# Adaptive layer-norm FFN, 1 core: condition slice 0 asked for in halves on two DMA queues, transposes and x tiles between the weight pieces

## The reference

```python
masked_w = weight * mask[None, :, :]                  # weight 8 x 512 x 512
w_bot = jnp.einsum('bg,got->bot', y, masked_w)        # y = cond_8, 2 x 8
h = jnp.einsum('bnt,bot->bno', x, w_bot) + bias
# _weight_quant: scale = 1/mean|w|, round(w*scale) clipped to -1..1, divided by scale
# _act_quant: scale = 127/max|row|, round(x*scale), divided by scale
gate = jax.nn.silu(_bitlinear(h, w_gate))             # 512 -> 2048
up = _bitlinear(h, w_up)                              # 512 -> 2048
return x + _bitlinear(gate * up, w_down)              # 2048 -> 512
```

## Time and profile before

| | |
|---|---|
| median of 3 runs | 454.75 us (453.04 to 455.91) |
| profiled execution, its own time | 453.42 us |
| its span | 451.6 us |
| PE busy | 434.9 us (96%) |
| DVE busy | 366.4 us (81%) |
| ACT busy | 327.1 us (72%) |
| POOL busy | 154.4 us (34%) |
| granted PE clock | full in every slice |

### The profile page before, as it was taken

The page is one execution under the profiler, slowest core; times in us unless marked ns, Lnnn a source line. Parts: engine busy times, 40 slices in busy tenths (PEclk is TensorE's granted clock), DMA queues, the critical chain, the costliest instruction groups (busy, mean ns, idle before and its releaser), DMA issues.

```text
span 451.6 us, 7215 instructions
## 1 busy us (share of the span) xinstructions
PE 434.9 (96%) x2186; PEld 232.7 (52%) x2186; DVE 366.4 (81%) x625; ACT 327.1 (72%) x448; POOL 154.4 (34%) x160
## 2 busy tenths in 40 slices
PE   4899998999999999999999999999999999999995
PEld 0234443444444455555655555655556565555654
DVE  0316579898956798799998999999999989999991
ACT  1216847785356776888888888888888888888861
POOL 0000170606099554232424324233341434414122
PEclk9999999999999999999999999999999999999999
DMA  7999997995420434352634526345353553535455
GB/s 281 402 401 415 412 252 160 339 279 121 102 48 10 78 77 109 103 116 77 159 69 134 119 75 150 67 133 118 91 134 75 141 107 103 116 93 142 86 148 139
DMA packets 104458, 69.78 MB, mean 155 GB/s; under 512 B 87281, under 2 KB 87537, under 8 KB 102897
## 3 DMA queue, kind: packets, MB, share of 16 engines
q1 hardware_dynamic: 103856, 67.39, 54.3%
q10 hardware_dynamic: 576, 2.10, 1.3%
HBM read 40.11 MB, written 8.39 MB: 107 GB/s over the span
## 4 chain that ended last, share of the span: by engine, by line
PE 44%; DMA 23%; DVE 12%; issue 11%; ACT 8%; SPq 1%; DVEq 0%; ACTq 0%
PE ps L888 12%; DMA wc<-wc 12%; PE ps L843 10%; PE ps L951 8%; PE ps L923 7%; DMA wc<-w_gate 4%; PE ps L881 4%; ACT wc L473 4%; DVE wc L733 3%; DVE wc L699 3%; DMA qT<-q_sb 3%; DMA wc<-wcond 2%; DMA wc<-w_down 2%; DVE p_part L751 2%; PE ps L856 1%
## 5 line engine op out<-in xcount | busy, mean ns | idle before, releaser
L888 PE MATMUL ps<-tern_up,qT 128*128 128x512 f16 x512 | 131.2, 379 | 0.6 <-DVE wc L733 0.6
L843 PE MATMUL ps<-w_bot,xT_sb 128*128 128x512 f32 x256 | 113.2, 595 | 2.3 <-DVE w_bot L636 1.6
L843 PEld LDWEIGHTS ps<-w_bot,xT_sb 128*128 128x128 f32 x256 | 48.0, 190 | 61.2 <-issue 57.5
L751 DVE TENSOR_REDUCE p_part<-wc 128x1 f32<-128x1536 f32 x64 | 77.9, 1218 | 1.7
L888 PEld LDWEIGHTS ps<-tern_up,qT 128*128 (+1 forms) x512 | 50.0, 98 | 55.3 <-DVE wc L733 1.3
L733 DVE TENSOR_TENSOR wc<-ps,xT_sb 128x512 f32<-128x512 f32 x104 | 71.3, 685 | 7.5 <-issue 3.6
L473 ACT ACTIVATE wc<-wc 128x1024 f16<-128x1024 f32 x64 | 67.0, 1051 | 4.6 <-DVE wc L796 2.8
L463 ACT ACTIVATE wc<-wc,p_scale 128x2048 f32<-128x2048 f32 x31 | 62.1, 2002 | 4.5 <-DVE p_scale L789 4.5
L951 PE MATMUL ps<-wc 128*128 128x256 f16 x480 | 62.2, 273 | 0.2 <-DVE wc L699 0.2
L699 DVE TENSOR_TENSOR wc<-wc 128x1024 f16<-128x1024 f16 x60 | 56.7, 945 | 3.8 <-DMA wc<-wc 2.7
L458 ACT ACTIVATE xT_sb<-ps,gate_unit 128x512 f32<-128x512 f32 x78 | 49.2, 684 | 11.7 <-PE ps L923 11.2
(11 more groups left out here) (93 smaller groups left out, 544.1 us busy)
## 6 DMA issues: line engine op xcount, KB each, us to landing
xT_sb<-xT SPq DMA_DIRECT2D x32, 256.0 KB, 7.5
x_res<-x SPq DMA_DIRECT2D x30, 256.0 KB, 2.9
out<-result SPq DMA_DIRECT2D x30, 256.0 KB, 2.4
wc<-wcond SPq DMA_DIRECT2D x12, 512.0 KB, 13.6
wc<-w_gate SPq DMA_DIRECT2D x4, 1024.0 KB, 17.7
wc<-w_up SPq DMA_DIRECT2D x4, 1024.0 KB, 13.4
wc<-w_down SPq DMA_DIRECT2D x4, 1024.0 KB, 7.3
wc<-wcond ACTq DMA_DIRECT2D x4, 512.0 KB, 7.7
```

The lines of the kernel that those rows point to most:

```text
L751: nc.vector.tensor_reduce(p_part[:, par, i:i + 1], prod[:, par, 512 * lo:512 * hi], AX.X, ALU.max, apply_absolute_value=True).then_inc(par ...
L843: ins = nc.tensor.matmul(ps[:, t % COND_BANKS], xT_sb[:, t % XSLOTS, k], w_bot[:, t // HALF, k], start=(k == 0), stop=(k == KH - 1))
L888: ins = nc.tensor.matmul(ps[:, UP + i % 2], tile_of(s, k), tern_up[:, i, k], start=(k == 0), stop=(k == KH - 1))
```

## The change

1. ACT asks for pieces 0 and 1 of condition slice 0 alone, and SP for pieces 2 and 3, behind `y_col` and in front of the first mask and the x tiles 0 to 2.
2. SP asks for the x tiles 8 to 10 between w_gate's pieces 1 and 2 (before: behind piece 3). Each of these loads waits for a tile of PE, and gate 2 and 3 are behind them.
3. SP asks for the transposes of tiles 0 to 3 between the pieces of w_up, and for the masks and x tiles 12 to 14 there too (before: masks and x tile 11 between up 1 and 2, all transposes behind up 3). AHEAD is 11 for 12.
4. ACT sums gate 0 and 1, then rounds tile 0, sums gate 2, rounds tile 1, sums gate 3, and rounds tile 2 (before: all four sums first).
5. `abs_total(0)` goes from ahead of tile 8 to ahead of tile 9, and its bank from 2 to 3.

```diff
-AHEAD = 12
+AHEAD = 11
-SUM_TILE = (8, 14, 21)
-SUM_BANK = (10 % 8, 16 % 8, 23 % 8)
+SUM_TILE = (9, 14, 21)
+SUM_BANK = (11 % 8, 16 % 8, 23 % 8)
...
             sp.dma_start(y_sb[:, :], y_col).then_inc(s_small, 16)
+            for i in range(2, 4):
+                sp.dma_start(wc[:, 0, 2 * i:2 * i + 2], wcond[0, :, 2 * i:2 * i + 2]).then_inc(s_wc[0][i], 16)
             load_wc(0)
...
-            for a in range(PIECES):
-                if a % 2 == 0:
-                    sp.wait_ge(mix_psum, 2 * (a // 2 + 1))
-                load_raw(0, w_gate, a)
-            for a in range(PIECES):
-                if a % 2 == 0:
-                    sp.wait_ge(mix_psum, 2 * (a // 2 + 3))
-                if a == 0:
-                    for t in range(XSLOTS, XSLOTS + 3):
-                        load_xT(t)
-                if a == 2:
-                    for k in range(KH):
-                        load_mask(1, k)
-                    for t in range(XSLOTS + 3, AHEAD):
-                        load_xT(t)
-                load_raw(1, w_up, a)
-            for t in range(LATE):
+            sp.wait_ge(mix_psum, 4)
+            load_raw(0, w_gate, 0)
+            load_raw(0, w_gate, 1)
+            for t in range(XSLOTS, XSLOTS + 3):
+                load_xT(t)
+            load_raw(0, w_gate, 2)
+            load_raw(0, w_gate, 3)
+            load_xT(XSLOTS + 3)
+            sp.wait_ge(mix_psum, 2 * KH)
+            load_raw(1, w_up, 0)
+            transpose_q(0)
+            load_raw(1, w_up, 1)
+            transpose_q(1)
+            for k in range(KH):
+                load_mask(1, k)
+            load_xT(XSLOTS + 4)
+            transpose_q(2)
+            load_raw(1, w_up, 2)
+            load_xT(XSLOTS + 5)
+            transpose_q(3)
+            load_raw(1, w_up, 3)
+            load_xT(XSLOTS + 6)
+            for t in range(QSLOTS, LATE):
...
-            for i in range(4):
+            for i in range(2):
                 nc.scalar.dma_start(wc[:, 0, 2 * i:2 * i + 2], wcond[0, :, 2 * i:2 * i + 2]).then_inc(s_wc[0][i], 16)
...
-            for a in range(PIECES):
-                abs_sum_piece(0, a)
-            abs_after = {3: (1, 0), 4: (1, 1), 5: (1, 2), 6: (1, 3), 12: (2, 0), 13: (2, 1), 14: (2, 2), 15: (2, 3)}
+            abs_sum_piece(0, 0)
+            abs_sum_piece(0, 1)
+            abs_after = {0: (0, 2), 1: (0, 3), 3: (1, 0), 4: (1, 1), 5: (1, 2), 6: (1, 3), 12: (2, 0), 13: (2, 1), 14: (2, 2), 15: (2, 3)}
```

## The result

| | before | changed |
|---|---|---|
| median of 12 runs | 453.40 us (452.71 to 455.91) | 455.74 us (453.43 to 457.59) |
| profiled execution, its own time | 453.42 us | 454.06 us |
| its span | 451.6 us | 452.3 us |

The ratio of the times is 1.0046, with a 95% interval of 1.0032 to 1.0060: the changed kernel is slower by 0.46%, about 2.1 us (the medians lie 2.3 us apart). I had forecast a gain of 0.9 us. The profiled execution lies near the lower end of its kernel's runs and shows 0.7 us of it; the other part is looked for in the experiments.

A forecast was written before the change was run, and what follows sets the result against it. DMA was taken as full from 6 to 56 us, PE as leading from 128 us. Front 0, tile 16 -0.55 and `abs_total(2)` -0.33 make -0.9 us: 453.9 us from a 454.75 median, range 451.4 to 457.4.

The forecast's parts named there:

- gate 2 is then issued at 40.8, before gate 1 lands, so the queue need not run empty: DMA queue between w_gate's pieces 1 and 2: no gap; if it ran empty, up to half a microsecond later.
- rival C: Gate pieces: gate 2 lands 1 to 2 us later than 45.6, tile 16 +0.45 to +1.45, 454.9 to 455.9 us; chance 0.12.
- The bytes ahead of gate 2: Three x tiles, 0.79 MB, ahead of gate 2 take 1.9 to 2.0 us, so it lands at 45.6 for 43.6.
- POOL's start: POOL's scaling of w_gate starts 0.55 to 0.6 us earlier, at 54.7 us.
- tile 16: PE's tile 16, which waits for DVE's mean of w_up, starts at 79.24 us for 79.79, -0.55 us.
- The 0.33 us at `abs_total(2)`: PE no longer waits at its last abs_total, near 97 us: -0.33 us.
- the longer stand at this place: PE, ready earlier, stands 1.5 us for the mean of w_up ahead of tile 16 instead of 0.64.
- The front: Condition slices and mixing: PE's head start from slice 0 is spent in waits for slices 1 and 2; gain 0.
- rival A: DMA starts better in its first 6 us or gate 2 comes earlier: 452.3 us, down to 451.5; chance 0.2.
- D: The halves don't bring slice 0 earlier, as SP's queue starts late: 453.9 us as well; chance 0.55 together with the forecast.
- Rival B: SP is held by issuing the transposes, up 3 lands at 74.7 us: +3.8 us, 458.5 us; chance 0.1.
- The sum of up 3: ACT's sum of w_up's last piece ends at 68 to 69.7 us, before PE asks at 70.6, so hidden.

The follow-up runs named there:

- the second: The changed kernel with condition slice 0 asked for by ACT alone, as before the change: 454.84 us, ratio 1.0012 to the kernel before.
- the eleventh experiment: The changed kernel with gate pieces in a row, abs_total(0) back ahead of tile 8 and ACT's order as before: 455.60 us, ratio 1.0054.
- the eighth: The changed kernel run once more without an edit: 456.22 us, ratio 1.0051; its section also counts low-clock executions across the kernels.

## Why the prediction was wrong

**The step that failed** is in part 2: "gate 2 is then issued at 40.8, before gate 1 lands, so the queue need not run empty". The issue time was off by 0.8 us (41.61), since PE was 0.9 us later out of its mixing; the landing was off by 2.1. What was wrong is the conclusion. I took gate 1's landing, 41 us, for the time until which the queue has work. It is the time of the slowest of 16 engines; by the DMA share most of the others were without work from about 38 us, 3.6 us before gate 2 was issued. The sum had an empty queue at nothing; I allowed for half a microsecond of it beside the sum and for 1 to 2 us in rival C; gate 2 was 2.1 us later than 45.6 (47.7), and 3.9 in the repeat. The bytes ahead of gate 2, the term that I did count, were about right: masks of the same size in this place put its sum at 45.1.

**The sum.** POOL's start was put at -0.6 and measured +1.34. Everything behind it followed as predicted: the ternary piece, the mean of w_up and tile 16 moved by +1.1, where I had written -0.55. The 0.33 us at `abs_total(2)` were won (17.24 for 17.55 us). +1.13 - 0.31 = +0.8 us, and the span showed +0.7. That is rival C, with its tile 16 at +0.45 to +1.45 as far as its path goes. That the measured median, 455.74, also lies in its 454.9 to 455.9 us is luck: these were counted from 454.75, the median of three runs of the kernel before, where twelve give 453.40. From there C says 453.5 to 454.5, which fits the executions at full clock (454.3) and not the median.

**What C did not contain** is the clock. With PE standing 2.4 us and more ahead of tile 16, many executions lose some 1.7 us more, as the rows of the second and the eleventh experiment show at just this place. For the changed kernel itself only the mean clocks of its timed runs show it; that the fall is at tile 16 there too is argued from those two and from the counts under the eighth. I had written the longer stand at this place down as free, an effect of PE being early.

**The front** came out as forecast: +0 from the halves, the head start spent in waits for slices 1 and 2 (the waits lie within the mixing, 2.78 and 2.96 us for 1.92 and 2.17). Between two kernels that differ only here nothing can be told, 451.16 and 451.09 us. In the first 4 us of the queues' work the DMA moved 256 GB/s for 247, so a second issuing queue hardly started it better. The rule of the Trainium skill ("DMA: Bandwidth & Descriptors", section "Issuing engines are not separate DMA queues") that the prediction weighed agrees with that. So rival A fell, and D too: slice 0 was there 2.0 us earlier. Slice 2 landed 0.9 us later than forecast, but PE's exit from the mixing varies as much between profiles of one front (34.8 to 35.7 us without halves, 35.2 to 35.8 with them), so whether the halves cost a few tenths there stays open.

**SP and the transposes.** Rival B fell: the issue of tile 1's transpose took 1.23 us at 51.04, not 5.86. The sum of up 3 ended at 69.8 us, where the forecast had 68 to 69.7, and PE did not wait for it at 71.31.

**Open** is why gate 2, issued at 41.3 to 41.6 us behind three small loads, took 6.1 us to land in one execution and 8.2 in another of the same kernel (in the first the share from 40 to 41 us was 0.61 at 33 GB/s, so the engines counted as busy while few bytes moved), what makes up the other 1.2 us between the two groups of executions, and what besides the length of a stand decides whether the clock falls.

## What to carry to other kernels

A load that waits for an engine should stand in a DMA queue behind those that wait for nothing, and a queue's reserve is counted from where most of the DMA engines run dry, not from where the last piece lands: read the DMA share per 2 us around such a wait, not the landing. A reordering whose parts depend on each other is worth nothing by halves: ACT's order alone gave 0, and with the gate pieces in a row SP's order lost 0.5% without ACT's and won 0.6% with it. And a stand of PE that only takes up slack is not free once it is a few microseconds long: most executions of the kernels with such stands had a lower mean clock.

## What the runs showed of the hardware

- In the changed kernel the last 1 MB load ahead of the hole was down to two or three engines' worth of the 16 for the last 2 to 3 us before its landing (share 0.15, 61 GB/s from 38 to 40 us, landing at 40.55).
- PE's granted clock fell to the 1.2 GHz level at stands of 2.68, 2.72 and 4.54 us (0.53 and 0.62 from 82 to 86 us; 0.71, 0.50 and 0.94 from 80 to 86; 0.50 from 100 to 106), and did not at one of 3.15 us. The first two falls cost 1.7 us each over 40 matmul records (19.10 and 19.08 us for 17.41).
- While POOL scaled w_up, DVE's two instructions on a gate piece took 1.51 us for 1.21 and 2.35 us for 0.69, in one execution; that POOL is the reason is argued.
